# Two attention layers on one core: image rows taken in runs of 128, ones multiplied ahead of the first weights, a new order before t, P tiles in a ring of 16, and a new order of maxima and of the last attention

## What is computed

```python
xn = group_norm(x, gamma, beta)             # 32 groups of 8 channels, over all positions of an image
q, k, v = xn @ wq + bq, xn @ wk + bk, xn @ wv + bv
attn = softmax(q @ k.T / sqrt(256))         # 1024 x 1024 for each image
x = (attn @ v) @ wp + bp + x
```

## Time and profile before

| | |
|---|---|
| median of 3 runs | 272.69 us (272.2 to 272.89) |
| the profiled execution | 271.55 us, of which the profile's span is 269.6 |
| PE busy | 257.4 us, 95% of the span |
| PEld, DVE, ACT, POOL busy | 232.8, 172.5, 151.1, 110.5 us |
| chain that ended last | PE 75%, DVE 8%, ACT 8%, issue 6% of the span |
| `attend`, three matmuls x 256 each | 218.3 us of PE busy time |
| `scores`, three matmuls x 128 each | 151.4 us of PE busy time |

### The profile page before, as it was taken

One profiled execution on the slowest core, in us unless ns is written; L12 is line 12 of the kernel. 1 busy time (PEld: TensorE's weight loads), 2 busy tenths in 40 slices (PEclk: granted clock), 3 DMA queues, 4 the chain that ended last, 5 costly groups with the idle time before them and its releaser, 6 DMA issues.

```text
span 269.6 us, 4591 instructions
## 1 busy us (share of the span) xinstructions
PE 257.4 (95%) x1650; PEld 232.8 (86%) x1650; DVE 172.5 (64%) x436; ACT 151.1 (56%) x295; POOL 110.5 (41%) x111
## 2 busy tenths in 40 slices
PE   3899899999999999999999999999999999999994
PEld 2788689889988899879998899879998899889993
DVE  0599576786687557475977557475977547454613
ACT  3465454499778507670687606680577507670750
POOL 2015300187345914451255813461065724550680
PEclk9999999999999999999999999999999999999999
DMA  5960000000000000000000000000110000100102
GB/s 136 368 239 1 0 1 0 2 0 2 0 1 0 4 2 0 0 1 2 0 1 2 0 2 0 0 0 2 40 41 0 4 19 19 39 2 19 58 3 78
DMA packets 5965, 7.37 MB, mean 27 GB/s; under 512 B 556, under 2 KB 4664, under 8 KB 5944
## 3 DMA queue, kind: packets, MB, share of 16 engines
q1 hardware_dynamic: 5920, 7.08, 7.8%
q10 hardware_dynamic: 24, 0.01, 0.0%
HBM read 4.99 MB, written 2.10 MB: 26 GB/s over the span
## 4 chain that ended last, share of the span: by engine, by line
PE 75%; DVE 8%; ACT 8%; issue 6%; DMA 1%; POOL 1%; DVEq 0%; ACTq 0%; POOLq 0%
PE ring L953 10%; PE ring L955 10%; PE ring L954 10%; PE ring L914 9%; PE ring L916 9%; PE ring L915 9%; PE ring L900 3%; PE ring L901 3%; PE ring L902 3%; ACT S L401 2%; PE Z L812 2%; ACT P_hi L400 2%; PE ring L887 2%; PE ring L888 2%; PE ring L889 2%
## 5 line engine op out<-in xcount | busy, mean ns | idle before, releaser
L286 POOL TENSOR_TENSOR P_lo<-S,P_hi 128x512 fp32r<-128x512 f32 x64 | 82.9, 1302 | 104.3 <-ACT S L401 104.3
L953 PE MATMUL ring<-V,P_hi 128*128 128x258 f32 x256 | 73.6, 287 | 0.0
L955 PE MATMUL ring<-V,P_lo 128*128 128x258 f32 x256 | 72.4, 283 | 0.0
L954 PE MATMUL ring<-V,P_hi 128*128 128x256 f32 x256 | 72.3, 282 | 0.0
L393 ACT COPY S<-ring 128x512 f32<-128x512 f32 x64 | 37.6, 587 | 37.4 <-PE ring L916 34.6
L914 PE MATMUL ring<-t_hi,xn_lo 128*128 128x512 f32 x128 | 51.4, 402 | 0.8 <-DVE t_lo L607 0.8
L400 ACT ACTIVATE P_hi<-S 128x512 fp32r<-128x512 f32 x64 | 40.7, 635 | 19.3 <-DVE S L642 17.7
L916 PE MATMUL ring<-t_hi,xn_hi 128*128 128x512 f32 x128 | 50.1, 391 | 0.0
L915 PE MATMUL ring<-t_lo,xn_hi 128*128 128x512 f32 x128 | 49.9, 390 | 0.0
L954 PEld LDWEIGHTS ring<-V,P_hi 128*128 128x128 f32 x256 | 48.5, 189 | 0.5
L953 PEld LDWEIGHTS ring<-V,P_hi 128*128 128x128 f32 x256 | 48.4, 189 | 0.5
(11 more groups left out here) (100 smaller groups left out, 350.3 us busy)
## 6 DMA issues: line engine op xcount, KB each, us to landing
xnat<-in_x SPq DMA_DIRECT2D x8, 256.0 KB, 6.7
out<-xnat SPq DMA_DIRECT2D x16, 128.0 KB, 1.9
wide<-in_vectors SPq DMA_DIRECT2D x2, 384.0 KB, 6.9
w_wq<-in_L_conv_wq SPq DMA_DIRECT2D x2, 256.0 KB, 4.8
w_wk<-in_L_conv_wk SPq DMA_DIRECT2D x2, 256.0 KB, 4.9
w_wv<-in_L_conv_wv SPq DMA_DIRECT2D x2, 256.0 KB, 6.5
w_wp<-in_L_conv_wp SPq DMA_DIRECT2D x1, 256.0 KB, 6.5
w_wp<-in_L_conv_wo SPq DMA_DIRECT2D x1, 256.0 KB, 6.8
```

The costliest lines, as they stand in the source:

```text
L286: nc.gpsimd.tensor_tensor(P_lo[:, tile, :], S[:, tile, :], P_hi[:, tile, :].bitcast(F32), ALU.subtract).then_inc(po_P, 1)
L953: nc.tensor.matmul(bank[:, 0:C + 2], P_hi[:, tile, mine], v[:, kb, 0:C + 2], start=(kb == 0), stop=False)
L954: nc.tensor.matmul(bank[:, 0:C], P_hi[:, tile, mine], v[:, kb, C + 2:VX], start=False, stop=False)
L955: last = nc.tensor.matmul(bank[:, 0:C + 2], P_lo[:, tile, mine], v[:, kb, 0:C + 2], start=False, stop=(kb == NB - 1))
```

## The change

The image is read and written with partition p holding tokens p, 128 + p, 256 + p and so on. Each row load then takes two runs of 128 tokens of 1 KB each, where it took 128 pieces of 2 KB with a step of 8 KB.

PE multiplies ones by ones six times into Z (`keep_running`), behind one new DVE memset, before it waits for the constants and wq. The work in front of the first t has another order on PE, ACT and DVE; output bias 1 goes between the two halves of t, and Wx(1) behind t. The P tiles get a ring of 16, so exponentials of a chunk wait for the attention two chunks back. On ACT all eight exponentials of a first chunk stand ahead of the score copies of the second. `query_shift` is cut in two: `query_maxima` (the reduction) and the rest. In `attention`, `maxima_by_query` moves from behind j = 0 to within it (behind kb = 4), and `shift_to_all` from behind j = 1 to behind (j, kb) = (1, 1). The group mean and variance of the next unit move from behind scores 4 and 6 to behind scores 2 and 4, and DVE's share of them earlier as well. The next unit's first half of t comes behind j = 1 and not j = 2. The last attention goes by keys for kb = 0 to 3, then by queries for kb = 4 to 7. The diff, cut to its core:

```diff
-    x_rows = x.rearrange("b (p k) c -> b p k c", k=NB)
+    x_rows = x.rearrange("b (k p) c -> b p k c", k=NB)
-    out_rows = out.rearrange("b (p k) c -> b p k c", k=NB)
+    out_rows = out.rearrange("b (k p) c -> b p k c", k=NB)
+    def exp_of(c, kb):
+        return (c * NB + kb) % P_TILES
...
-            ring_order += [("O", 2 * u, j) for j in range(3)]
+            ring_order += [("O", 2 * u, j) for j in range(2)]
             ring_order += [("t", u + 1, 0, k) for k in range(KC)]
-            ring_order += [("O", 2 * u, j) for j in range(3, QB)]
+            ring_order += [("O", 2 * u, j) for j in range(2, QB)]
...
@@ ACT
             def exponentials(c, kb):
-                if c * NB + kb >= TILES:
-                    act.wait_ge(pe_O, ((c * NB + kb - TILES) // NB + 1) * QB)
+                if c > 1:
+                    act.wait_ge(pe_O, (c - 1) * QB)
...
-                t_high(u, 1, 0)
-                exponentials(first, 0)
-                t_high(u, 1, 1)
-                exponentials(first, 1)
-                exponentials(first, 2)
-                if more:
-                    raw_rows(u + 1, 2, Z)
-                exponentials(first, 3)
+                for kb in range(NB):
+                    if kb in (3, 4):
+                        t_high(u, 1, kb - 3)
+                    if more and kb == 6:
+                        raw_rows(u + 1, 2, Z)
+                    exponentials(first, kb)
@@ DVE
+            nc.vector.memset(R[:, 0:P], 1.0).then_inc(dv_ones, 1)
...
+            for r in range(NR):
+                statistics_of(0, r)
+            channel_statistics(0)
+            group_deviation(0)
             A_low(0, 0)
+            variance(0)
             A_low(0, 1)
+            affine_map(0)
+            normalise(0, range(0, 2))
+            xn_low(0, 0)
+            xn_low(0, 1)
             attention_vector(0, 0)
             attention_vector(0, 1)
+            normalise(0, range(2, 4))
+            for k in range(KC):
+                Wx_low(0, k)
+            xn_low(0, 2)
+            xn_low(0, 3)
+            for k in range(KC):
+                t_low(0, 0, k)
+            for k in range(KC):
+                A_low(1, k)
+            attention_vector(0, 2)
+            for k in range(KC):
+                t_low(0, 1, k)
+            for l in range(LAYERS):
+                output_bias(l)
+            for k in range(KC):
+                Wx_low(1, k)
+            for n in range(NATT):
+                attention_vector(1, n)
...
@@ PE
+            def keep_running(n):
+                for _ in range(n):
+                    nc.tensor.matmul(Z[:, 0:P], R[:, 0:P], R[:, 0:P], start=True, stop=True)
+            pe.wait_ge(dv_ones, 1)
+            keep_running(6)
...
             mean_of_groups(0)
             Wx_product(0, 0)
             variance_of_groups(0)
             Wx_product(0, 1)
-            transpose_weight(1, 2)
+            transpose_weight(1, 0)
+            transpose_weight(1, 1)
             pe.wait_ge(dv_stat, VARE)
-            for l in range(LAYERS):
-                output_bias(l)
+            output_bias(0)
             for mc in range(KC):
                 A_product(1, mc)
-            pe.wait_ge(ac_wT, 6)
-            for mc in range(KC):
-                Wx_product(1, mc)
+            transpose_weight(1, 2)
+            for k in range(KC):
+                t_product(0, 0, k)
+            output_bias(1)
+            for k in range(KC):
+                t_product(0, 1, k)
+            for mc in range(KC):
+                Wx_product(1, mc)
...
                     for kb in range(NB):
                         attend(c, j, kb)
-                    if j == 0:
-                        maxima_by_query(following)
+                        if (j, kb) == (0, 4):
+                            maxima_by_query(following)
+                        if (j, kb) == (1, 1):
+                            shift_to_all(following)
                     if j == 1:
-                        shift_to_all(following)
                         before_third()
...
+                    if more and kb == 2:
+                        mean_of_groups(u + 1)
                     if more and kb == 4:
-                        mean_of_groups(u + 1)
-                    if more and kb == 6:
                         variance_of_groups(u + 1)
-                attention(first, second, lambda: None, next_first_half)
+                attention(first, second, next_first_half, lambda: None)
-            for kb in range(NB):
+            for kb in range(NB // 2):
                 attention_by_keys(CHUNKS - 1, kb)
+            pe.wait_ge(po_P, CHUNKS * NB)
+            for j in range(QB):
+                for kb in range(NB // 2, NB):
+                    attend(CHUNKS - 1, j, kb)
```

More of the change, by code:

```diff
@@ L463, in _ @@
                         xn_high(u + 1, q)
-                for kb in range(3):
+                for kb in range(6):
+                    if more and kb in (2, 3):
+                        t_high(u + 1, 0, kb - 2)
                     exponentials(second, kb)
[L466 to L470, removed]
+            for kb in range(6, NB):
                 exponentials(CHUNKS - 1, kb)
@@ L676, in _ @@
                     shifted(0, kb + 1)
+            query_maxima(1)
             query_shift(1)
+            for kb in range(2):
+                shifted(1, kb)
             for q in range(2):
                 xn_low(1, q)
-            for kb in range(2):
+            for kb in range(2, 4):
                 shifted(1, kb)
@@ L689, in _ @@
                     t_low(1, 0, j // 2)
-            for kb in range(4, 6):
-                shifted(1, kb)
             for u in range(1, UNITS):
@@ L715, in _ @@
-                shifted(first, 3)
+                shifted(first, 6)
+                shifted(first, 7)
                 output(before, 2)
-                shifted(first, 4)
                 if more:
                     statistics_of(u + 1, 2)
-                shifted(first, 5)
                 output(before, 3)
-                shifted(first, 6)
-                for kb in range(1, NB):
-                    running_max(second, kb)
-                    if kb == 1:
-                        shifted(first, 7)
-                        if more:
-                            statistics_of(u + 1, 3)
-                            channel_statistics(u + 1)
-                    if more and kb == 5:
-                        group_deviation(u + 1)
-                    if more and kb == 7:
-                        variance(u + 1)
+                if more:
+                    statistics_of(u + 1, 3)
+                    channel_statistics(u + 1)
@@ L735, in _ @@
+                running_max(second, 1)
+                running_max(second, 2)
+                if more:
+                    group_deviation(u + 1)
+                running_max(second, 3)
+                if more:
+                    variance(u + 1)
+                running_max(second, 4)
                 if more:
                     affine_map(u + 1)
+                running_max(second, 5)
+                if more:
+                    normalise(u + 1, range(1))
+                running_max(second, 6)
@@ L738, in _ @@
+                if more:
+                    normalise(u + 1, range(1, 2))
+                running_max(second, 7)
+                if more:
+                    normalise(u + 1, range(2, TQ))
+                query_maxima(second)
+                query_shift(second)
                 output(first, 0)
-                query_shift(second)
                 if more:
-                    normalise(u + 1)
                     xn_low(u + 1, 0)
                     xn_low(u + 1, 1)
-                output(first, 1)
@@ L745, in _ @@
                 shifted(second, 0)
                 shifted(second, 1)
+                if not more:
+                    shifted(second, 2)
+                    shifted(second, 3)
+                output(first, 1)
                 if more:
```

127 lines of the change are left out of this document (53 added, 74 removed).

## The result

The changed kernel takes 265.38 us (264.9 to 266.63, 4 runs) against 272.44 (271.52 to 272.89) in the same session: a ratio of 0.9752, 95% interval 0.9708 to 0.9796, so 7.1 us faster (5.6 to 8.0 by the interval) where 5.4 were forecast. The time lies in the range (265.3 to 269.8) by only 0.1 us, less than the executions scatter, so that it fell inside and not outside is luck. The profiled executions are 6.4 us apart (271.55 and 265.16, spans 269.6 and 263.3). The rest of the 7.1 is scatter: the profiled execution of before lies 0.9 us under its median.

A forecast was written before the change was run, and what follows sets the result against it. PE work bounds the long middle, so only its waits can be taken away. Front 2.2, first query shift 0.7, group variance 1.6 and last attention 0.9 sum to 5.4: 272.69 - 5.4 = 267.3 us, range 265.3 to 269.8.

The forecast's parts named there:

- Front: Work ahead of the first scores: they start 2.2 us earlier, by the new order, the ones and the faster row load.
- its bounds: Front gain by the row loads: 1.0 us if rows land as now, 3.4 if at wk's speed; middle taken.
- The 1.0 us that I gave the order together with the clock: Front with rows landing as now and PE's clock up at 7.85: first scores at 27.65 instead of 28.64.
- First query shift: At the first query shift, the reduction leaves the path; PE's wait of 0.8 falls to about 0.1: 0.7 us.
- Group variance: Units 2 and 3: ACT no longer late with score copies, so both PE waits go: 2 x 0.78 = 1.6 us.
- P ring and ACT's order: Exponentials and score copies on ACT: 16 P tiles free ACT, which was to remove the group variance waits, 1.6 us.
- Maxima and shift within the attention: Inside attentions, PE asks for R and the shift with 0.45 us slack at both: 0 us.
- Last attention: Last attention and end: only one output, not all four query blocks, follows PE's last matmul: 0.9 us.
- the clock was up: Front, against the rival that the clock is not up at 7.85: front -0.2, time 269.7 us; rival's chance 16%.
- DVE did not become the bound: Six attentions, against the rival that DVE is the next bound: 270.3 us, or 268.8 at half; chance 10%.
- the hold by POOL: Six attentions: rival that POOL's P_lo holds DVE's small steps, adding 12.4 us, time 279.7; chance 4%.
- More than forecast: Front: rival that rows land at wk's speed (266.1) and PE's wait and clock share are smaller, to 265; chance 8%.

The follow-up runs named there:

- late statistics: Changed kernel with group mean and variance behind scores 4 and 6, DVE's share as late, next unit's t behind j = 2: 271.71 us, ratio 0.9994.
- one place later: Changed kernel with group_deviation one running maximum later on DVE (behind that of scores 3 instead of 2): 266.65 us, ratio 0.9814.
- ACT's old order: Changed kernel with exponentials 4 to 7 of a first chunk between the second chunk's score copies, P ring of 16 kept: 268.56 us, ratio 0.9873.
- shift_late: Changed kernel with maxima behind j = 0 and shift behind j = 1 as before: 266.97 us, ratio 0.9816.

## Why the prediction held, by its own steps

**PE bounds the middle.** Right. 237.0 us became 234.2, and in the six kernels whose edit touched only front or end it stayed 234.2 to 234.3.

**Front, 2.2 us.** 2.42 in the profiled pair (28.64 to 26.22). The layout was taken halfway between its bounds and the clock as up; the runs show that the front gained from both, 1.7 and 0.7 us by medians (1.6 and 0.6 by ratios), and the speed of the transposes confirms the clock. The 1.0 us that I gave the order together with the clock is not tested as such: with both others taken back the order gives 0.1 us in the traces and about 0.4 by medians, at the lower speed, for which I had -0.2. The first row pair came at 5.70, close to wk's speed; the second one then stopped PE for 0.89 us, which I had not foreseen.

**First query shift, 0.7 us.** Ahead of `shift_to_all(0)` PE loses 0.13 us instead of 0.80 (distance of its starts less the usual one): 0.67.

**Group variance, 1.6 us.** Both waits are gone, the size was 1.8, and the step's cause failed: "DVE came late because its running maximum waited 0.92 us for a score copy, ACT being behind". That the size came out right all the same is luck, since both waits went for another reason. The waits came back at the same length with ACT free (late statistics, one place later), and did not come back with ACT late (ACT's old order). What removed them is that DVE now has two blocks of scores, 2.8 us, for a chain of 1.9 us, where it had one, 1.39. The row with 0.92 us of idle time was read as lateness, but it is 0.91 in the run one place later too, with ACT in time: it is the normal wait for the next block.

**P ring and ACT's order, 0 by themselves.** I gave them the variance. They are worth 3.5 and more (the order) and 8.6 us (the ring, under that order) within the new kernel, but no run has them alone in the kernel before. The stretches in which a wait went (0.89 and 0.88 at the variances, 0.67 at the first shift, 0.15 at V of unit 1) are 2.6 of the 2.8 us of middle, so nothing of size is left that they could have won directly. What they do in the new kernel is pay for DVE's affine work between the maxima and for row copies in time, which would otherwise stop PE.

**Maxima and shift within the attention, 0.** With shift_late the middle is 1.7 us longer, of which 0.77 is the last P_lo that I had named as 1.5 us of slack bought by it; about 0.9 us I had counted as nothing.

**Last attention, 0.9 us.** 0.93 by the end window; another 0.2 us came from stores that land in 1.7 instead of 1.9 us, for which I had counted nothing.

**Sum.** 2.4 + 0.7 + 1.8 + 0.1 (V of unit 1, 0.32 to 0.21) + 1.1 = 6.1 of the 6.3 us of span; the 0.2 of the middle that are left lie in steps of 0.03 to 0.06 us over the attentions. The rivals: the clock was up; DVE did not become the bound; the hold by POOL did not occur at the six places that it was priced for. "More than forecast", at 8%, came nearest to the time, and only in part by its own reason: the rows landed near wk's speed, but the front gained 2.4 us and not 3.4. The rest are errors of the same sign in four terms, and 0.7 us of scatter between the profiled executions and the medians.

## What to carry to other kernels

Where PE is the bound, count for each of its questions to another engine how much PE work lies between the last input of the chain and the question, and compare it with the chain's length: a place one block earlier on DVE was worth 0.9 us each time, and a freer ACT nothing for these waits. An idle time ahead of an instruction does not say that its feeder is late; compare the feeder's start with the end of what it waits for. Parts of such a change lean on each other: the order on ACT without its 16 tiles made the kernel slower than before, so a single part tried alone can look like a loss.

## What the runs showed of the hardware

The loads of image 0 (256 KB each) ran faster as runs of 128 rows of 1 KB than as 128 pieces of 2 KB at a step of 8 KB: 278 to 361 GB/s in eleven traces against 131 to 184 in three, in the window from 5 to 6 us. The second image came at 413 GB/s with that same step; why only the first is slow stays open. The granted clock column is 1.00 in the front while transposes run at half their later rate (without the ones eight take 1.97 us at 6.38 and 1.04 us at 9.41), so there the spacing tells the speed and the column does not. The column fell to 0.57 behind one of two standstills of 3.1 us. A short stop of PE shown as 0.62 us cost 0.9. The Trainium skill (SBUF — State Buffer, Who interferes with whom) says that a VectorE instruction with two SBUF inputs contends with a GpSimd one that reads SBUF. The trace agrees, down to instructions of 4 columns: 1.27 us instead of 0.16 beside a subtraction of 1.28.
